# Cross attention: maxima kept in bf16 and spread by one product, column sums from two bf16 halves, output weights in eight pieces

## The reference

```python
# x: layer-normed draft, c: context
q = rope(rms_norm(x @ Wq.T) * q_norm_w)                 # 16 heads
k = rope(rms_norm(concat(c, x) @ Wk.T) * k_norm_w)      # 4 heads, 1857 keys
v = concat(c, x) @ Wv.T
probs = softmax(q @ k.T / sqrt(128))                    # over all keys
out = (probs @ v) @ Wo.T                                # added to the residual
```

## Time and profile before

| | |
|---|---|
| median of 3 runs | 1650.81 us (1650.22 to 1650.82) |
| the profiled execution's own time | 1648.11 us |
| its span | 1646.3 us |
| mean granted clock of TensorE | 0.966 |
| busy: PE, DVE, ACT, POOL | 1470.2, 1287.7, 1029.3, 1127.9 us |
| the attention stage, 447 to 1565 us: busy PE, DVE, ACT, POOL | 1073.16, 908.32, 775.49, 939.34 of 1118 us |

### The profile page before, as it was taken

One profiled execution on the slowest core, in us unless ns is written; L12 is line 12 of the kernel. 1 busy time (PEld: TensorE's weight loads), 2 busy tenths in 40 slices (PEclk: granted clock), 3 DMA queues, 4 the chain that ended last, 5 costly groups with the idle time before them and its releaser, 6 DMA issues. The chain is left out here.

```text
span 1646.3 us, 25844 instructions
## 1 busy us (share of the span) xinstructions
PE 1470.2 (89%) x8223; PEld 855.8 (52%) x8332; DVE 1287.7 (78%) x2581; ACT 1029.3 (63%) x2439; POOL 1127.9 (69%) x1033
## 2 busy tenths in 40 slices
PE   6598697757778999999999999989999999999988
PEld 5477365533544555455455555545545555554455
DVE  7876577878569888787977888887887878878766
ACT  3364464744366777676677766676776766766552
POOL 2363471112459789988978998888898878877742
PEclk9799798979899999999999999999999999999999
DMA  3000831020000001000000100000000000000020
GB/s 102 1 2 2 296 114 39 1 73 0 32 1 14 14 1 41 14 1 1 1 1 1 28 14 1 1 1 1 14 28 1 1 1 1 1 1 1 1 59 26
DMA packets 30991, 38.47 MB, mean 23 GB/s; under 512 B 4996, under 2 KB 26504, under 8 KB 30856
## 3 DMA queue, kind: packets, MB, share of 16 engines
q1 hardware_dynamic: 30856, 36.82, 6.9%
HBM read 35.76 MB, written 1.05 MB: 22 GB/s over the span
## 5 line engine op out<-in xcount | busy, mean ns | idle before, releaser
L2168 POOL TENSOR_TENSOR stream_acc<-stream_acc,stream_weights 128x512 f32<-128x512 f32 (+1 forms) x374 | 491.9, 1315 | 80.6 <-ACT stream_weights L2059 59.0
L1988 PE MATMUL stream_banks<-stream_weights,stream_v 128*128 128x512 f32 (+1 forms) x876 | 451.6, 600 | 0.0
L2240 DVE TENSOR_TENSOR stream_most<-stream_most,stream_banks 128x512 f32<-128x512 f32 (+1 forms) x416 | 284.9, 685 | 157.4 <-ACT stream_weights L2053 142.2
L2053 ACT COPY stream_weights<-stream_banks 128x512 f32<-128x512 f32 (+1 forms) x438 | 256.6, 586 | 238.8 <-PE stream_banks L1956 231.0
L2059 ACT ACTIVATE stream_weights<-stream_weights 128x512 f32<-128x512 f32 (+1 forms) x438 | 278.5, 637 | 60.2 <-DVE stream_weights L2226 57.6
L2226 DVE TENSOR_TENSOR stream_weights<-stream_weights,stream_banks 128x512 f32<-128x512 f32 (+1 forms) x438 | 297.0, 680 | 2.8 <-PE stream_banks L1977 1.5
L2175 POOL TENSOR_TENSOR stream_by_cos<-stream_by_cos,stream_by_sin 128x256 f32<-128x256 f32 x192 | 135.8, 728 | 88.4 <-DVE stream_by_sin L2282 88.2
L1956 PE MATMUL stream_banks<-stream_q_t_lo,stream_k_t_hi 128*128 128x512 bf16 (+1 forms) x479 | 181.7, 379 | 9.2 <-DVE stream_most L2240 3.1
L1956 PE MATMUL stream_banks<-stream_q_t_hi,stream_k_t_lo 128*128 128x512 bf16 (+1 forms) x480 | 182.1, 379 | 0.1
L1956 PE MATMUL stream_banks<-stream_q_t_hi,stream_k_t_hi 128*128 128x512 bf16 (+1 forms) x388 | 147.6, 381 | 15.5 <-DVE stream_most L2240 14.8
L1988 PEld LDWEIGHTS stream_banks<-stream_weights,stream_v 128*128 128x128 f32 (+1 forms) x876 | 144.0, 191 | 29.7 <-issue 5.3
(11 more groups left out here) (445 smaller groups left out, 3099.6 us busy)
## 6 DMA issues: line engine op xcount, KB each, us to landing
memory_raw_t<-in_ctx_t SPq DMA_DIRECT2D x4, 1601.0 KB, 9.1
memory_raw<-in_ctx SPq DMA_DIRECT2D x4, 1536.0 KB
row_ctx_t<-in_ctx_t SPq DMA_DIRECT2D x6, 512.0 KB, 3.7
early_raw<-in_L_xattn_Wq SPq DMA_DIRECT2D x4, 512.0 KB, 3.8
early_raw<-in_L_xattn_Wo SPq DMA_DIRECT2D x4, 512.0 KB, 3.9
row_ctx_t<-in_ctx_t SPq DMA_DIRECT2D x1, 1601.0 KB, 7.0
moe_raw_up<-in_L_ffn_wi SPq DMA_DIRECT2D x6, 256.0 KB, 4.3
model_x<-in_x SPq DMA_DIRECT2D x1, 1024.0 KB, 5.4
```

The source lines that it names most:

```text
L1988: nc.tensor.matmul(ps[:, 2 + n, :], v[0:r, g % 2, t, :], room(step)[0:r], start=(t == 0), stop=(t == KT - 1)).then_inc(weighed, 1)
L2053: nc.scalar.copy(room(step)[0:r], ps[0:r, step % 2, :]).then_inc(copied, 1)
L2168: nc.gpsimd.tensor_tensor(acc[0:r, h % 2, :], acc[0:r, h % 2, :], room(step)[0:r], ALU.add).then_inc(acc_ready, 1)
L2240: nc.vector.tensor_tensor(most[0:r], most[0:r], ps[0:r, step % 2, :], ALU.max).then_inc(maxed, 1)
```

## The change

The running maximum `most` becomes bf16, and `turn_most` transposes it with the bf16 identity into a bf16 view of bank 6. `turn_top`, `flatten`, the table `own` and its load and cast are gone. A new VectorE operation, `place_top`, in slot 1 after `lower`, writes `tops`: the bf16 identity times `top`, both repeated, a 128 x 512 tile with each block's maxima on its diagonal. The spread is one product of it with `less`, 128 x 128 of −1, into bank 7.

For the sums, ScalarE copies `acc` to bf16 (`split_high`, slot 6, after its exponential), VectorE subtracts that from `acc` into a second bf16 half (`split_low`, slot 6, right after `keep_most`), and `sum_up`, now in slot 7, multiplies both halves' blocks with a bf16 column of ones: eight products for four columns. `invert` moves to slot 7 too. The last pass keeps its f32 sums.

The output weights come in eight loads of two heads each into half of `raw` (the two bf16 halves lie in the other half), copied by ScalarE in slots 8 and 17 of a group and subtracted by VectorE in slots 12 and 22.

```diff
+def sums_in(slot):
+    return [h for h in pass_at(slot, SUM_LATE + 1) if h < PASSES - 1] + [h for h in pass_at(slot, SUM_LATE) if h == PASSES - 1]
+def splits_in(slot):
+    found = [("sum", h) for h in pass_at(slot, SPLIT_LATE) if h < PASSES - 1]     # SPLIT_LATE = SUM_LATE
...
-        most = sb("most", [P, HALF])
+        most = sb("most", [P, HALF], BF16)
+        tops = sb("tops", [P, 4, P], BF16)
+        turned_most = ps[:, 6, :].bitcast(BF16)[:, 0:HALF]
+        raw_o = raw[:, 0:512].rearrange("p (h n) -> p h n", h=2)
+        halves = [raw[:, 512 + 256 * i:768 + 256 * i].bitcast(BF16) for i in range(2)]
...
 turn_most:
-    last = nc.tensor.transpose(ps[:, 6, c * P:(c + 1) * P], most[:, c * P:(c + 1) * P], const["ident"][:])
+    last = nc.tensor.transpose(turned_most[:, c * P:(c + 1) * P], most[:, c * P:(c + 1) * P], const["ident_b"][:])
-def turn_top(h):  ...
-def flatten(h):  ...
 spread:
-    pe.wait_ge(flat_ready, h + 1)
+    pe.wait_ge(tops_ready, h + 1)
     if h >= 1:
         pe.wait_ge(lowered, STEPS * h)
-    for c in range(4):
-        last = nc.tensor.matmul(ps[:, 7, c * P:(c + 1) * P], own[:, c, :], flat, start=True, stop=True)
-    last.then_inc(spread_ready, 1)
+    nc.tensor.matmul(ps[:, 7, :], less[:], tops[:].rearrange("p c n -> p (c n)"), start=True, stop=True).then_inc(spread_ready, 1)
 sum_up:
-    pe.wait_ge(acc_ready, after_first(STEPS * (h + 1) - 1))
+    pe.wait_ge(split_lo, split_at["sum", h] + 1)
     for c in range(4):
-        last = nc.tensor.matmul(ps[:, 6, c:c + 1], acc[:, h % 2, c * P:(c + 1) * P], ones[:], start=True, stop=True)
+        for part in range(2):
+            last = nc.tensor.matmul(ps[:, 6, c:c + 1], halves[part][:, c * P:(c + 1) * P], ones_b[:],
+                                    start=(part == 0), stop=(part == 1))
+def split_high(kind, n):                              # ScalarE, after exponent
+    ac.wait_ge(acc_ready, after_first(STEPS * (n + 1) - 1))
+    ac.wait_ge(sum_ready, before + 1)                 # the sums of the pass before
+    nc.scalar.copy(split_part(kind, n, 0), split_source(kind, n)).then_inc(split_hi, 1)
+def place_top(h):                                     # VectorE, slot 1, after lower
+    ve.wait_ge(top_ready, h + 1)
+    if h >= 1:
+        ve.wait_ge(spread_ready, h)
+    nc.vector.tensor_tensor(tops[:], bcast(const["ident_b"][:], 1, 4), bcast(top[:], 2, P), ALU.mult).then_inc(tops_ready, 1)
+def split_low(kind, n):                               # VectorE, after keep_most
+    ve.wait_ge(split_hi, split_at[kind, n] + 1)
+    nc.vector.tensor_tensor(split_part(kind, n, 1), split_source(kind, n), split_part(kind, n, 0), ALU.subtract).then_inc(split_lo, 1)
...
-    if 0 <= g < KVH and late == 8:                    # ScalarE, output weights
+    if 0 <= g < KVH and late in (8, 17):
-    if 0 <= g < KVH and late in (17, 22):             # VectorE
+    if 0 <= g < KVH and late in (12, 22):
```

More of the change, by code:

```diff
@@ L1642, in cross_attention @@
         ones = sb("ones", [P, 1])
-        own8 = sb("own8", [8, 8])
-        own = sb("own", [4, 4, P], BF16)
+        less = sb("less", [P, P], BF16)
+        ones_b = sb("ones_b", [P, 1], BF16)
         half = sb("half", [P, 4])
@@ L1734, in cross_stream @@
         inv = spare[:, DC * CTX - 8:DC * CTX]
-        flat = spare[0:4, DC * CTX - 128:DC * CTX - 64].bitcast(BF16)
         SPARE_ROOMS = DC * CTX // HALF - 4
@@ L1843, in cross_stream @@
         for s in SLOTS:
-            for kind, items in (("tops", pass_at(s, TOPS_LATE)), ("flat", pass_at(s, FLAT_LATE)), ("turn", turns_in(s)),
-                                ("sum", pass_at(s, SUM_LATE)), ("out", outs_in(s))):
+            for kind, items in (("tops", pass_at(s, TOPS_LATE)), ("turn", turns_in(s)),
+                                ("sum", sums_in(s)), ("out", outs_in(s))):
                 for item in items:
@@ L1849, in cross_stream, with split_source, split_part @@
                     bank6_before[kind, item] = freed
-                    freed = {"tops": lambda: (top_ready, item + 1), "flat": lambda: (flat_ready, item + 1),
+                    freed = {"tops": lambda: (top_ready, item + 1),
                              "turn": lambda: (lo_ready, item + 1), "sum": lambda: (inv_ready, item + 1),
                              "out": lambda: (added, QT * (PAIR * item[0] + item[1] + 1))}[kind]()
+        split_hi, split_lo = sem("split_hi"), sem("split_lo")
+        splits = [item for s in SLOTS for item in splits_in(s)]
+        split_at = {item: n for n, item in enumerate(splits)}
+        def split_source(kind, n):
+            return acc[:, n % 2, :] if kind == "sum" else room(n)[0:rows_of(n % STEPS)]
+        def split_part(kind, n, part):
+            return halves[part] if kind == "sum" else halves[part][0:rows_of(n % STEPS)]
         with nc.Block() as block:
@@ L2028, in _ @@
                         turn_most(h)
-                    for h in pass_at(slot, FLAT_LATE):
-                        turn_top(h)
                     for u in turns_in(slot):
                         turn(u)
-                    for h in pass_at(slot, SUM_LATE):
+                    for h in sums_in(slot):
                         sum_up(h)
@@ L2095, in high @@
                     nc.scalar.copy(place(0, u), turned_heads(u)).then_inc(hi_ready, 1)
[L2097 to L2101, removed]
+                def split_high(kind, n):
+                    if kind == "sum":
+                        ac.wait_ge(acc_ready, after_first(STEPS * (n + 1) - 1))
+                    else:
+                        ac.wait_ge(p_ready, n + 1)
+                    if split_at[kind, n] >= 1:
+                        kind_before, before = splits[split_at[kind, n] - 1]
+                        if kind_before == "sum":
+                            ac.wait_ge(sum_ready, before + 1)
+                        else:
+                            ac.wait_ge(weighed, before + 1)
+                    nc.scalar.copy(split_part(kind, n, 0), split_source(kind, n)).then_inc(split_hi, 1)
                 def att_high(h):
@@ L2113, in _ @@
                         exponent(slot - LOWER)
+                    for kind, n in splits_in(slot):
+                        split_high(kind, n)
                     for h in pass_at(slot, ATT_LATE):
@@ L2319, in _ @@
                         lower(slot - LOWER)
+                    for h in pass_at(slot, TOPS_LATE + 1):
+                        place_top(h)
                     for h in pass_at(slot, ATT_LATE + 1):
@@ L2330, in _ @@
                         keep_most(slot)
+                    for kind, n in splits_in(slot):
+                        split_low(kind, n)
                     if 0 <= slot - WEIGH < ALL:
                         accumulate_rest(slot - WEIGH)
-                    for h in pass_at(slot, SUM_LATE):
+                    for h in sums_in(slot):
                         invert(h)
```

54 lines of the change are left out of this document (23 added, 31 removed).

## The result

The changed kernel takes 1709.3 us (median of 4 runs, 1707.43 to 1710.15) against 1650.78 before: ratio 1.0354, interval 1.0336 to 1.0372. It is slower by 58 us. The profiled execution took 1710.15, its span is 1708.4, so its span is 62.1 longer than before; the mean granted clock is .942 (.966).

What follows compares the result with a forecast made beforehand. TensorE's instruction stream plus its stands was taken as the bound. Profiled 1648.1, waits +40.2 (−12.5+52.8−.1) and clock +12 gave 1700; with the runs' median 2.7 higher, 1702 was forecast, likeliest 1685 to 1718, full range 1655 to 1722.

Steps and rivals of the forecast that it cites:

- Pass starts, −12.5: bf16 maxima and one spread product: TensorE gains .70 per pass, less waits for the last lowering; −12.5 us in all.
- long starts: The 17 pass starts with a projection of .65 in between; claimed to keep the whole .70.
- 12 short ones: Pass starts without a projection in slot 1; place_top late behind GpSimd's power, so about .2 of .70 stays.
- Sums, +52.8: TensorE waits in slot 7 for split_high and split_low: 14×2.75 + 14×.7 + 3×1.5, bf16 products priced .50.
- two kinds of stand: TensorE's waits for split_low before the sum: about 3 us at 14 query places, about 1 at 14 others.
- query places: The 14 passes where VectorE rotates a query tile in slot 6; score of slot 8 later by 2.75 us each.
- GpSimd beside split_low: Split_low, with two SBUF operands, waits for GpSimd's additions; at query places +2.75 with that wait, +2.0 without.
- The rival without this wait: Split_low and place_top cost .60, no wait for GpSimd, no clock fall: +12.7, 1664 us; chance .17.
- The clock, +12: Granted clock falls after 3 us stands at query places, 1.7 us each, between 0 and 24; half taken.
- Output weights, 0: Eight pieces copied by ScalarE are hidden: zero; a late piece would cost about 5 us once in project_out.
- the sum is hidden: Split_low done when TensorE ends slot 7's score: −34, 1617 us; half kept gives 1634; together chance .10.
- key passes: The 14 passes of the other kind; score of slot 8 forecast +.7 each, pass length about unchanged.

Runs made afterwards that it cites:

- filled stands: Changed kernel with products nobody reads before sum_up's wait for split_low, 13 at query places, 4 at the other kind: 1684.37 us, ratio 1.0219 to the kernel before.

## Why the prediction was right

It said 1702, slower with .85, for two stands of 3.1 and about 1 us at the sums and for falls of the clock after the long ones. All three are there. By its terms, measured as ratios of the runs times 1650.8 (the terms add up to 1703; the forecast rounded down):

- *Pass starts, −12.5*: measured −10 (.9939). Right in total, by two errors that offset. The .70 holds at the long starts (35.20 to 34.48 us a pass). Of the .5 that the 12 short ones were to lose, because place_top would wait for GpSimd's power, only .16 is lost (32.11 to 31.55 us a pass; place_top takes .68 beside the power). But the spread waits 12.7 us for the lowering, where 3.8+1.8 were reckoned: 4.00, 2.46 and 2.46 in three starts with angle work on VectorE, and .70 to 1.08 in four others. In the first of them place_top is struck by GpSimd's addition, 1.81 at 516.15 in the changed kernel. Moving it to ScalarE returned 7 us by the medians.
- *Sums, +52.8, the clock apart*: the sums cost 58.4+10.1 = 68.5 us in all; filled stands leave 46 of them. The two kinds of stand are as worked out (mostly 3.09 and 1.10, against 3.1 and .9). The mis-sized term is the price of the eight bf16 products, .20 against .50, 31×.30 = 9 us too dear; the sentence on the Trainium skill ("TensorE: Matmul & The Clock Gate", "Weight-path perf modes"), by which the sum would be nearer .22, is what the trace bears out. So the waits for split_low come to 68.1 us, where 50 to 60 were forecast: at most query places they are 3.08 to 3.48, and two are 5.04 and 5.05 us, where VectorE also splits the next batch's context in slot 5 (L2400, 1.92 us).
- *GpSimd beside split_low*: predicted to stretch it to 1.2 to 1.4, measured 1.30, and 17.5 us. The rival without this wait (+12.7, 1664) is refuted for split_low; place_top was not stretched in 27 of 32 passes. The page "SBUF — State Buffer" of the Trainium skill, section "SBUF: two separate sides", names the two-operand lock against GpSimd operations that read SBUF; split_low agrees (1.30 with two SBUF operands, .69 with one), place_top beside the 128x4 power (.68) does not show it. Where place_top runs first, GpSimd pays: its next operation (L2210) takes 1.50 to 1.52 at nine long starts, as at 1369.86, and 1.04 behind place_top at 1334.61.
- *The clock, +12*: measured 22. The step "of the two stands one was followed by a fall; I take half" failed: 13 of 14 query places fell. The trace of before had two long stands to go by, too few for a share. The price of one fall was right in most places, 1.7 forecast and 1.69 measured in the two passes compared above.
- *Output weights, 0*: measured 1.0003.
- *The rival "the sum is hidden"* named its own point: split_low done by the time TensorE ends the score of slot 7. Made in slots 4 and 5 it is done by then, the stands and the falls at the sums are gone, and still no gain of 34 follows, but 5 (.9972). The key passes do gain 1.33 us (35.20 to 33.87). The query passes gain only .35, because the score of slot 8 there waits for VectorE's maximum of slot 6, and the six passes with angle or context work lose. The prediction, like the rival, priced VectorE's added operations at nothing as long as VectorE's total (28 to 30 us) is below TensorE's; that holds in the key passes, and fails where VectorE rotates a query tile in slot 6 or has angle or context work.

So the 58 us are: −10 at the pass starts, +46 of standing at the sums net of their shorter products, +22 of clock. GpSimd's part of the last two is 17.5. What stays open: why the one query place at 1419 kept its clock after the same stand, and how the loss of the early halves in the six passes with angle or context work splits into waits and clock.

## What to carry to other kernels

A cheaper instruction on the saturated engine is no gain if it needs operands that two other engines must first make: place the preparation by when its input is final (here two slots earlier), not by where the old instruction stood. Price a new operation on an engine with spare time slot by slot, where others wait for it, not by its total: the early split_low cost nothing in a key pass, about .2 us in a query pass, and the most in the passes in which VectorE had other work. And count a stand of TensorE with what the clock loses after it: products that nobody read made this kernel 22 us faster.

## What the runs showed of the hardware

- Eight bf16 one-column products with 128-column weights take .20 us from their start to that of the next product, where four f32 ones took .81.
- A VectorE operation with two SBUF operands took .68 beside a GpSimd power on 128x4 that lasts 1.01 us, but 1.30 to 1.35 beside GpSimd additions of 128x512, and up to 1.81 at 516.15 (the addition beside it is 1.26 long).
- Where the VectorE operation starts first, the GpSimd operation is the longer one: L2210 (128x512) took 1.50 to 1.52 us beside place_top nine times, and 1.04 in all but two of its other places.
- After stands of 3.08 to 5.05 us the granted clock fell 13 times in 14, after the stands of .49 to 2.23 us at the other sums it stayed at 1.00; in the two us from 1350 it was .52, half of full speed for nearly all of them.
